# Causal attention: GpSimd issues the stack transfers, and the first keys are transposed in another PSUM bank

## The reference

```python
q = jnp.einsum('bsm,hmd->bshd', resid, W_Q) + b_Q     # k and v likewise
q = _apply_rotary(q, sin, cos, ROT_DIM)
k = _apply_rotary(k, sin, cos, ROT_DIM)
k = jnp.concatenate([k, virtual_k])                   # 512 + 16 keys; v likewise
scores = jnp.einsum('bqhd,bkhd->bhqk', q, k) / SCALE
mask = arange(kv_len)[None, :] <= arange(s)[:, None] + VKV
pattern = softmax(where(mask, scores, -inf))
z = jnp.einsum('bhqk,bkhr->bqhr', pattern, v_g)       # 8 value columns a head
out = jnp.einsum('bqhd,hdm->bqm', z, W_O)
```

## Time and profile before

| | |
|---|---|
| median of 3 runs | 1702.01 us (1699.63 to 1706.09) |
| the profiled execution | 1699.04 us, its span 1697.2 us |
| mean granted TensorE clock | 0.948 of full speed |
| TensorE busy | 1473.9 us, 87% |
| VectorE busy | 1234.0 us, 73% |
| ScalarE busy | 1119.9 us, 66% |
| GpSimd busy | 440.1 us, 26% |
| DMA, SyncE's queue | 270.63 MB, 56.3% of 16 engines' span |
| the causal attention's units | about 72 to 641 us of the span |

### The profile page before, as it was taken

The page is one execution under the profiler, slowest core; times in us unless marked ns, Lnnn a source line. Parts: engine busy times, 40 slices in busy tenths (PEclk is TensorE's granted clock), DMA queues, the critical chain, the costliest instruction groups (busy, mean ns, idle before and its releaser), DMA issues. The chain is left out here.

```text
span 1697.2 us, 36694 instructions
## 1 busy us (share of the span) xinstructions
PE 1473.9 (87%) x12580; PEld 938.1 (55%) x12580; DVE 1234.0 (73%) x3703; ACT 1119.9 (66%) x2657; POOL 440.1 (26%) x442
## 2 busy tenths in 40 slices
PE   4688998989989885588888888769999999999996
PEld 2255555556555553366666666646555555555564
DVE  4367777777777765688888788663877878878755
ACT  1267676776767761567777677627888787887742
POOL 0333333333333313454544444330000000000001
PEclk9599999999999997899999999877999999999998
DMA  1677777788777745111001110007999999999920
GB/s 41 163 185 194 188 186 197 185 194 190 186 186 189 194 108 187 22 30 31 19 20 31 25 27 19 12 13 219 324 315 315 309 314 300 313 314 302 292 73 25
DMA packets 154904, 272.97 MB, mean 161 GB/s; under 512 B 27920, under 2 KB 31200, under 8 KB 154592
## 3 DMA queue, kind: packets, MB, share of 16 engines
q1 hardware_dynamic: 154720, 270.63, 56.3%
HBM read 148.03 MB, written 112.98 MB: 154 GB/s over the span
## 5 line engine op out<-in xcount | busy, mean ns | idle before, releaser
L519 ACT ACTIVATE a_Pm<-a_Pm,a_nm 128x272 f32<-128x272 f32 (+3 forms) x512 | 266.7, 570 | 167.3 <-DVE a_nm L441 166.7
L441 DVE CUSTOM_DVE_ANT_0 a_Pm<-ps,a_mask 128x272 f32<-128x272 f32 (+3 forms) x512 | 237.7, 503 | 92.3 <-PE ps L358 90.8
L1768 ACT COPY r_BD<-ps 128x320 f32<-128x320 f32 x512 | 200.4, 428 | 92.1 <-PE ps L1621 46.7
L1895 DVE CUSTOM_DVE_ANT_0 r_Sx<-ps,r_Sx 128x512 f32<-128x512 f32 x256 | 176.8, 691 | 108.8 <-PE ps L1634 107.2
L1621 PE MATMUL ps<-r_R,r_qv 32*128 32x320 f32 x1024 | 234.2, 498 | 3.2 <-ACT r_BD L1768 2.3
L358 PE MATMUL ps<-a_Kst,a_Qst 128*128 128x272 f32 (+4 forms) x640 | 200.6, 409 | 15.4 <-DMA a_Kst<-bounce 15.1
L1634 PE MATMUL ps<-r_K,r_qu 32*128 32x256 f32 x1024 | 199.7, 436 | 3.4 <-DVE r_nb L1895 3.4
L358 PEld LDWEIGHTS ps<-a_Kst,a_Qst 128*128 128x128 f32 x640 | 113.4, 193 | 146.3 <-issue 62.6
L1775 ACT ACTIVATE r_Sx<-r_Sx,r_nb 128x512 f32<-128x512 f32 x256 | 187.6, 733 | 7.9 <-DVE r_nb L1895 7.9
L1904 DVE COPY r_PT<-ps 128x512 f32<-128x512 f32 x256 | 175.9, 687 | 4.6 <-PE ps L1644 4.0
L373 PE MATMUL ps<-m_ident,a_Pm 128*128 128x128 f32 x1280 | 170.5, 278 | 1.6 <-ACT a_Pm L519 0.7
(11 more groups left out here) (204 smaller groups left out, 2745.9 us busy)
## 6 DMA issues: line engine op xcount, KB each, us to landing
spill<-r_BD SPq DMA_DIRECT2D x256, 288.0 KB, 5.0
r_Sx<-spill SPq DMA_DIRECT2D x128, 512.0 KB, 5.7
a_Kst<-bounce SPq DMA_DIRECT2D x128, 264.0 KB, 4.9
a_Qst<-bounce SPq DMA_DIRECT2D x128, 256.0 KB, 4.6
bounce<-a_kh SPq DMA_DIRECT2D x32, 264.0 KB, 3.5
bounce<-a_kl SPq DMA_DIRECT2D x32, 264.0 KB, 4.1
bounce<-a_qh SPq DMA_DIRECT2D x32, 256.0 KB, 5.7
bounce<-a_ql SPq DMA_DIRECT2D x32, 256.0 KB, 6.0
```

The source lines that it names most:

```text
L441: nc.vector.tensor_tensor_reduce(out=Pm[:, u % 2, qt, 0:w], in0=S[:, S_of[qt]:S_of[qt] + w], in1=mask[:, N + AV - w:N + AV], scale=-SCALE, ...
L519: nc.scalar.activation(row, row, ACT.Exp, scale=-1.0, bias=nm[:, u % 2, qt:qt + 1]).then_inc(exp_done, 1)
L1768: nc.scalar.copy(BD[:, m % BUFS, j, HW * half:HW * half + HW], ps[:, BDB[k % 3], 0:HW]).then_inc(bd_ev, 1)
L1895: nc.vector.tensor_tensor_reduce(out=row, in0=ps[:, AC + n % 2, :], in1=row, scale=-SCALE, scalar=-BIG, op0=ALU.add, op1=ALU.min, accum_ou ...
```

## The change

`stack` is split in two. `to_memory` stays on SyncE and only writes the bounce. The wait for the landed bounce and the four stack DMAs go to a new `stack` on GpSimd. In the first step GpSimd issues `stack(0, m - 1)` after the low half of `m`, and `stack(0, 3)` at the end; in the loop it issues a pair's stack at the even unit that follows the odd unit in which the low half was made, ahead of that unit's `first_keys`. The one semaphore `bounced` becomes four, one for each `m`. The semaphores `stk` are made in the caller and are not cleared at the end of the attention.

`first_transposes` writes to bank TB + 1 and waits for VectorE's evacuation of it, no more for ScalarE's; `first_evacuate` reads that bank. The wait for that evacuation moves from the transposes into bank TB (`k == 0`) to those into TB + 1 (`k == 1`), which come first in a unit.

```diff
-            def stack(st, m):
+            def to_memory(st, m):
                 i, k = m // 2, 4 * st + m
                 width_ = (N, KN)[m % 2]
-                dst, halves = ((Qst, (qh, ql)), (Kst, (kh, kl)))[m % 2]
+                halves = ((qh, ql), (kh, kl))[m % 2]
                 for j, (src, made) in enumerate(zip(halves, (hi_done, lo_done))):
                     sp.wait_ge(made, k + 1)
-                    sp.dma_start(bounce[st % 2][m][j, :, 0:width_], src[:, i].bitcast(F32)).then_inc(bounced, 16)
-                sp.wait_ge(bounced, 32 * (k + 1))
-                if st >= 2:
-                    sp.wait_ge(s_ready, 2 * (U * (st - 2) + GH * (i + 1)))
-                for block, j in enumerate(((0, 1, 0, 1), (0, 0, 1, 1))[m % 2]):
-                    sp.dma_start(dst[st % 2][32 * block:32 * block + 32, :, i].bitcast(F32),
-                                 bounce[st % 2][m][j, :, 0:width_].rearrange("(h c) n -> c h n", h=GH)).then_inc(stk[st % 2][i], 16)
+                    sp.dma_start(bounce[st % 2][m][j, :, 0:width_], src[:, i].bitcast(F32)).then_inc(bounced[m], 16)
...
                 if k >= 4:
-                    pool.wait_ge(bounced, 32 * (k - 3))
+                    pool.wait_ge(bounced[m], 32 * st)
...
+            def stack(st, m):
+                i = m // 2
+                dst = (Qst, Kst)[m % 2]
+                width_ = (N, KN)[m % 2]
+                pool.wait_ge(bounced[m], 32 * (st + 1))
+                if st >= 2:
+                    pool.wait_ge(s_ready, 2 * (U * (st - 2) + GH * (i + 1)))
+                for block, j in enumerate(((0, 1, 0, 1), (0, 0, 1, 1))[m % 2]):
+                    nc.gpsimd.dma_start(dst[st % 2][32 * block:32 * block + 32, :, i].bitcast(F32),
+                                        bounce[st % 2][m][j, :, 0:width_].rearrange("(h c) n -> c h n", h=GH))\
+                        .then_inc(stk[st % 2][i], 16)
+
             for m in range(4):
                 add_pair(0, m)
                 split_lo(0, m)
+                if m >= 1:
+                    stack(0, m - 1)
+            stack(0, 3)
             for k in range(UNITS):
                 st = k // U + 1
                 if k % 2 == 1 and st < STEPS:
                     add_pair(st, k % U // 2)
+                if k % 2 == 0 and k >= 2 and (k - 2) // U + 1 < STEPS:
+                    stack((k - 2) // U + 1, (k - 2) % U // 2)
                 first_keys(k)
                 if k % 2 == 1 and st < STEPS:
                     split_lo(st, k % U // 2)
...
                     pe.wait_ge(exp_done, 4 * u + 4)
                     if u >= 1:
                         pe.wait_ge(evd, u)
+                    if u >= GH and u % GH == 1:
+                        pe.wait_ge(p0_ev, u // GH)
                 elif u >= 1:
                     pe.wait_ge(eva, 2 * u - (1 if k == 2 else 0))
-                if k == 0 and u >= GH and u % GH == 1:
-                    pe.wait_ge(p0_ev, u // GH)
...
                 pe.wait_ge(p0_done, GH * (bb + 1))
-                pe.wait_ge(eva, 2 * min(GH * (bb + 1) + 1, UNITS))
+                pe.wait_ge(evd, min(GH * (bb + 1) + 1, UNITS))
                 for qt in range(NT):
-                    ins = nc.tensor.transpose(ps[:, TB, P * qt:P * qt + P], P0[:, bb % 2, qt, :], c["ident"][:])
+                    ins = nc.tensor.transpose(ps[:, TB + 1, P * qt:P * qt + P], P0[:, bb % 2, qt, :], c["ident"][:])
...
-                nc.vector.tensor_copy(P0T[:], ps[:, TB, :]).then_inc(p0_ev, 1)
+                nc.vector.tensor_copy(P0T[:], ps[:, TB + 1, :]).then_inc(p0_ev, 1)
...
-    clear(nc, [*names, *stk[0], *stk[1]])
+    clear(nc, [*names, *bounced])
```

More of the change, by code:

```diff
@@ L190, in causal_attention, with attention_groups @@
             clear(nc, names)
-        attention_groups(nc, s, zd, sd, ps, c, d, xnT, V, V0, own, W, bias, vk, mask)
-def attention_groups(nc, s, zd, sd, ps, c, d, xnT, V, V0, own, W, bias, vk, mask):
+        attention_groups(nc, s, zd, sd, ps, c, d, stk, xnT, V, V0, own, W, bias, vk, mask)
+def attention_groups(nc, s, zd, sd, ps, c, d, stk, xnT, V, V0, own, W, bias, vk, mask):
     STEPS = AG * B // NB
@@ L220, in attention_groups @@
     names = (w0, w1, pj_ready, stt_done, added, hi_done, lo_done, s_ready, nm_ready, exp_done, t_done, evd, eva, pv_done,
-             tab_in, pad_done, ones_done, p0_done, p0_tr, p0_ev, vm_done, z_ready, z_ev, z0, z1, bounced) = s.sems(
+             tab_in, pad_done, ones_done, p0_done, p0_tr, p0_ev, vm_done, z_ready, z_ev, z0, z1) = s.sems(
         *("w0 w1 pj_ready stt_done added hi_done lo_done s_ready nm_ready exp_done t_done evd eva pv_done "
-          "tab_in pad_done ones_done p0_done p0_tr p0_ev vm_done z_ready z_ev z0 z1 bounced").split())
+          "tab_in pad_done ones_done p0_done p0_tr p0_ev vm_done z_ready z_ev z0 z1").split())
     w_in, z_out = (w0, w1), (z0, z1)
+    bounced = s.sems(*(f"bounced{m}" for m in range(4)))
     bounce = [[nc.dram_tensor(f"bounce{k}{m}", (2, P, KN), F32, kind="Internal").ap() for m in range(4)] for k in range(2)]
-    stk = [s.sems(f"stk{k}0", f"stk{k}1") for k in range(2)]
     STK = 16 * 2 * 4
@@ L277, in _ @@
             for m in range(4):
-                stack(0, m)
+                to_memory(0, m)
             for st in range(STEPS):
@@ L283, in _ @@
                     if st + 1 < STEPS:
-                        stack(st + 1, m)
+                        to_memory(st + 1, m)
                     if m % 2 == 0 and 2 * st + m // 2 >= 2:
@@ L2057, in program @@
         sd = nc.dram_tensor("sd", (B, AH, N), F32, kind="Internal").ap()
-        causal_attention(nc, X, zd, sd, ps, c, d)
+        stk = [s.sems(f"stk{k}0", f"stk{k}1") for k in range(2)]
+        causal_attention(nc, X, zd, sd, ps, c, d, stk)
         with ExitStack() as ctx_rw:
```

4 lines of the change are left out of this document (2 added, 2 removed).

## The result

The changed kernel takes **1722.62 us** (median of 4 runs, 1714.30 to 1726.31) against 1700.82 (1698.43 to 1706.09) for the kernel before in the same comparison: ratio **1.0117** [1.0073, 1.0161], slower by 22 us. Forecast was 1752: the right sign, a little over twice the size.

What follows compares the result with a forecast made beforehand. TensorE was taken to bound the kernel before, GpSimd's lengthened cycle the changed one. Cycle +51, start +4, tail −5 gave +50 on 1699.04, plus 3 to the median: 1752 us, range 1655 to 1820.

Steps and rivals of the forecast that it cites:

- the price X of a DMA issue on GpSimd: Four stack issues a pair on GpSimd: taken at 1.0 us each, between bounds of 0.44 and 2.35.
- the bounce's landing: GpSimd's wait from low half's end to landed bounce: 2.05 us, read at the quiet start and kept for the loop.
- The step on what bounds the kernel: Causal attention: TensorE leads, busy 453.4 of 500 us; SyncE's 265.7 us of bounce waits make transfers late, nearly all hidden.
- rival 1: GpSimd issues as cheaply as SyncE (up to 0.7 us), its cycle stays under TensorE's: 1660 us, chance 0.22.
- The cycle: GpSimd from low half to low half: 5.70 us plus four issues, 9.70 a pair against 8.83, +51 us.
- the floor I took: TensorE's work as the fastest possible pace of the attention: 8.2 us a pair.
- The estimate by the Trainium skill: GpSimd's DMA issue at about 0.84 us, from the skill's first-byte times; kernel time 1714 us.
- Start and tail: Attention's first steps: +4 us, issues delay first_keys(0); its end: −5 us, earlier last stack and no last L380 waits.
- The bank edit: First keys' transposes wait only for VectorE's evacuation: the 44.3 us at L380 go, not subtracted from the forecast.
- the cover that I named: Projection and three score matmuls hide the transposes' wait for L456's copy: priced 0, 21 us if the cover went.
- Rival 4: VectorE's copies of Vm lock GpSimd out of its port: at most +7 us, 1759; no chance of its own.
- Rival 3: TensorE's clock falls after waits, slowing two projections each time: +58 us, 1810 us, chance 0.05.

Runs made afterwards that it cites:

- e1: Kernel before with only the first keys' transposes moved to VectorE's bank, stacks still on SyncE: 1704.12 us, ratio 1.0017.
- e10: Kernel before, stacks on SyncE, first keys in ScalarE's bank, each stack reading and awaiting only last step's bounce (wrong scores): 1688.83 us, ratio 0.9953.
- e4: Changed kernel, stacks on GpSimd in place, each reading and awaiting only last step's bounce (wrong scores): 1635.94 us, ratio 0.9618.
- e11: Kernel before with first keys in VectorE's bank, SyncE's stacks reading and awaiting only last step's bounce (wrong scores): 1638.12 us, ratio 0.9646.
- e14: Kernel before with first keys in VectorE's bank; SyncE bounces both pairs of a half step, then issues both stacks: 1645.52 us, ratio 0.9701.
- e2: Changed kernel with the bank edit undone, so only the stacks on GpSimd remain: 1720.12 us, ratio 1.0109.
- e5: Changed kernel with first_keys of the even unit put ahead of the stack and its wait: 1714.63 us, ratio 1.0103.
- e6: Changed kernel with each stack DMA cut into two of half the columns, eight issues a stack, same bytes: 1810.78 us, ratio 1.0674.
- e7: Changed kernel with half the bytes in each stack from the third step on, same four issues: 1676.12 us, ratio 0.9887.
- e9: Changed kernel with GpSimd's stack issued a whole pair later: 1751.22 us, ratio 1.0331.
- e3: Changed kernel with GpSimd's stack one unit later, behind first_keys of the odd unit: 1698.30 us, ratio 0.9993.

## Why the prediction had the sign right and the size wrong

The step that failed is the price X of a DMA issue on GpSimd, taken at 1.0 us and measured at 0.55. A second term, the bounce's landing, was wrong the other way and hid two thirds of it.

**The step on what bounds the kernel was half wrong.** I read "TensorE leads" off the busy times and set the 265.7 us of the earlier trace rows aside as lateness "nearly all hidden". They were a second limit right behind the first. e1 (nothing gained with L380's waits gone), e10 (10 us gained with SyncE's wait gone and L380's left), and e4 and e11 (65 and 60 us with both gone) show it, and so does e14 (54 us), which waits for every bounce that it reads. It spoiled rival 1 above all: cheap issues alone were to give 1660. Issues were cheap, and the change still lost. The forecast itself it touched less, since that rested on GpSimd's cycle.

**The cycle was right, two of its terms were mis-sized.** e2, e5 and e6 show that the pace is the closed cycle from low half to low half.
- *X, one issue.* Taken 1.0, measured 0.55: 4 × 0.45 = 1.8 us a pair too much, +106 us in the sum. No run shows the 1.0. The price lay between my bounds (0.44 and 1.28), next to the near one: I leaned on GpSimd's 128x512 arithmetic at 1.28, and the like operation was SyncE's issue at 0.44.
- *Low half to landed bounce.* Taken 2.05 from the quiet start, measured 3.25 on average: +1.20 a pair, 71 us too little in the sum. I gave the reason in brackets, that a stack is through before the next bounce. It is not: the stack's landing takes 5.0 us from its issue, and e7 brings the wait back to 2.37 by halving its bytes. The other 0.3 us are no matter of bytes: GpSimd's wait stays 2.37 where the stack is out of the way (e6, e7), against SyncE's 2.05.

With both put right, 5.70 − 2.05 + 3.25 + 4 × 0.55 = 9.10, against 9.18 measured. The errors ran against each other, and that the sign came out right is luck: with X right and the landing left at 2.05, the cycle is 7.9, under the floor I took, and I would have forecast 1660.

The estimate by the Trainium skill ("DMA: Bandwidth & Descriptors", Specifications), X = 0.84 and 1714, came out nearer to the time than my own, by luck too: X was not 0.84, and the landing that it leaves at 2.05 makes up the difference. The figures of the Trainium skill are times to the first byte. How long an issue occupies its engine differs by 0.11 us here, 0.55 against SyncE's 0.44.

**Start and tail** came out at +3.5 (forecast +4) and −3 (−5). The tail went as said: unit 124 no longer waits for its stack. The start is the right number by another path. I had GpSimd's issues hold up `first_keys(0)`, which at 0.55 us each they do not: GpSimd is idle for 2.24 us before it. TensorE's first scores of the stage wait for the keys' first stack until 75.47 us instead of 72.19, since GpSimd issues that stack at 67.02, after the next pair's low half, and SyncE had issued it at 65.21.

**The bank edit** did to L380 what was said, and the cover that I named was the weak place: I priced the later wait for the copy of L456 at 0 as long as a projection and scores lie between. They still do, but the copy moved to 2.8 us behind, because VectorE's maxima ahead of it wait for GpSimd. e2 and e5 show that this cost nothing on top: the wait only changed its name. The edit is needed, though: 51 us of the gain in e11 against e10.

**Rival 4**, VectorE locking GpSimd out: no issue took over 0.77 us, and the 128 + 128 of them average 0.553 and 0.552. In the changed kernel that is no test, since none of the 32 copies of `Vm` runs beside an issue. In e4, 30 of them do, as here:
```profile
132.37 0.22 DVE L475 COPY a_Vm<-a_V 128x128 f32<-128x128 f32 x1
132.37 2.17 POOL L327 DMA_DIRECT2D a_Qst<-bounce  x4
```
All 30 issues took 0.55 us, and 29 of the 30 copies their usual 0.22 (the other began beside a low half). By the rule of the Trainium skill ("SBUF — State Buffer", SBUF: two separate sides) some should have been held up; this case doesn't show it. What does stand between issues are two holes of 2.24 us, 4.5 us in all. They go with the number of issues and not with VectorE: every run with four issues a stack on GpSimd has a hole (1.3 to 2.5 us) ahead of its 114th and its 210th issue, whenever that is; e6, with eight, has one ahead of the 114th and then of every 80th. What GpSimd does there is not shown.

**Rival 3**, the clock: 0.98 from 100 to 600 us against 1.00. TensorE's waits at L384, 1.8 us on average (52.5 over 29), cost little of it; those of e9, 2.8 on average, bring it to 0.94.

**Left open:** what fills the holes between issues. The gain of 60 us in e11 can't be split between loop and bank: alone they are worth 10 us (e10) and nothing (e1).

## What to carry to other kernels

- A queue that never waits for what it carries (here 1.6 us in 500), only for its own transfers, is a limit of the pace, however idle the engine behind it looks and however much busier TensorE is. A second limit can lie right on top of it: then neither is worth much alone, and both together are. Read a DMA queue's waits by whom they are for before the engines' busy times.
- A round trip through memory whose next leg is issued behind its own heavy transfer paces itself. Moving the wait to another engine, or later, keeps the loop or stalls that engine's program. Reordering so that only every second round trip is waited for, while other issues run, cuts it.
- A price of a transfer read at a quiet place (2.05 us) is a lower bound, not a value, for the same transfer in the loop (3.25 to 6.8 us here).

## What the runs showed of the hardware

- A plain DMA issue of 128 rows occupies GpSimd for 0.55 us, with rows of 1 KB or 2 KB (e6), against 0.44 for SyncE: cheap enough that 256 of them were free once nothing was waited for (e4).
- One part of a bounce (256 or 264 KB to memory) is there 2.0 to 2.4 us after its low half on quiet DMA engines, 3.25 with the rest of a stack in front, 6 to 6.8 right behind one. Putting the stack on GpSimd's queue and the bounce on SyncE's does not part them: in e3 it is still 6 us.
- The stacks' DMAs land in the same time from either queue: medians from 100 to 640 us of 5.0 and 4.7 us for keys and queries issued by GpSimd, 5.0 and 4.6 by SyncE.
- A 0.22 us copy on VectorE from SBUF to SBUF and a DMA issue on GpSimd run beside each other at full speed, 29 times in e4.
